# Last stage of a four-layer audio tower: GpSimd without the wait for the mixed heads' norm ahead of its second rest

## The reference, cut to what matters

```python
sx = einsum('bsh,ndh->bnsd', x, hl_w) + hl_b
q = einsum('bnsd,neod->bneso', sx, wq);  k = ...;  v = ...
att = softmax(einsum('bnesd,bntd->bnest', q, k) * d ** 0.5 + causal)
qkv = where(pad, 0.0, einsum('bnest,bntd->bnesd', att, v))
mixed = einsum('bnsed,bnse->bnsd', out, softmax(gates))
hn = layernorm(mixed + resid, ln_g, ln_b)          # the mixed heads' norm
fx = f_n.reshape(b, s, nh, d)
hx = relu(where(fx == 0, 0.0, fx @ fc1_w.T + fc1_b))
hx = where(fx == 0, 0.0, hx @ fc2_w.T + fc2_b)
hx = layernorm(hx + fx, fnorm_g, fnorm_b)          # the second norm
return h + hx * softmax(hx @ fgate_w.T)
```

## Time and profile before

| | |
|---|---|
| median of three runs | 3182.33 us |
| the profiled execution's own time | 3183.66 us |
| its span, first to last instruction | 3181.9 us |
| TensorE busy | 2969.3 us (93%) |
| VectorE busy | 2585.7 us (81%) |
| ScalarE busy | 1806.3 us (57%) |
| GpSimd busy | 1307.3 us (41%) |
| last stage, full rounds | about 2080 to 3040 us, 35 us each |
| draining rounds | about 3040 us to the end |
| TensorE's granted clock, 2080 to 3100 us | 1.00 |

### The profile page before, as it was taken

One profiled execution on the slowest core, in us unless ns is written; L12 is line 12 of the kernel. 1 busy time (PEld: TensorE's weight loads), 2 busy tenths in 40 slices (PEclk: granted clock), 3 DMA queues, 4 the chain that ended last, 5 costly groups with the idle time before them and its releaser, 6 DMA issues.

```text
span 3181.9 us, 72607 instructions
## 1 busy us (share of the span) xinstructions
PE 2969.3 (93%) x24964; PEld 2136.3 (67%) x24964; DVE 2585.7 (81%) x7699; ACT 1806.3 (57%) x4484; POOL 1307.3 (41%) x1368
## 2 busy tenths in 40 slices
PE   0699999999999979999799999999999999999995
PEld 0488888888888844444577777666666666666663
DVE  4788888888888658887778886688888888888873
ACT  0255555555555535555567775466666666666662
POOL 1435353545454324443100001356555555555542
PEclk9999999999999979999778988899999999999996
DMA  4100000000000000000000001432332233233210
GB/s 149 37 22 17 23 16 23 16 23 16 23 16 16 2 1 1 1 1 1 1 1 2 1 1 19 54 42 41 50 50 42 44 50 46 42 50 50 42 23 4
DMA packets 69714, 84.24 MB, mean 26 GB/s; under 512 B 19592, under 2 KB 64968, under 8 KB 68968
## 3 DMA queue, kind: packets, MB, share of 16 engines
q1 hardware_dynamic: 68328, 79.20, 13.8%
q10 hardware_dynamic: 1024, 0.39, 0.1%
HBM read 29.93 MB, written 3.17 MB: 10 GB/s over the span
## 4 chain that ended last, share of the span: by engine, by line
PE 34%; DVE 13%; POOL 2%; issue 2%; ACT 1%; DMA 0%; SPq 0%; POOLq 0%; DVEq 0%; ACTq 0%
PE psum L2310 4%; PE psum L2296 3%; PE psum L2324 3%; PE psum L2283 3%; PE psum L1641 3%; PE psum L2347 3%; DVE qe_top L2763 3%; PE psum L1670 2%; PE psum L1658 2%; POOL qe_root L3013 2%; DVE qe_y L2741 1%; PE psum L1712 1%; PE psum L1703 1%; PE psum L2259 1%; DVE qe_fo L2741 1%
## 5 line engine op out<-in xcount | busy, mean ns | idle before, releaser
L2763 DVE TENSOR_REDUCE qe_top<-psum 125x1 f32<-125x375 f32 (+2 forms) x896 | 499.4, 596 | 102.5 <-PE psum L2283 101.2
L2570 ACT ACTIVATE qe_E<-psum 125x375 f32<-125x375 f32 (+1 forms) x896 | 454.7, 531 | 210.7 <-PE psum L2283 203.7
L2283 PE MATMUL psum<-bconst 125*125 125x125 bf16 (+2 forms) x1792 | 466.5, 260 | 0.0
L606 PE MATMUL psum<-Q,K 96*125 96x125 f32 (+3 forms) x2304 | 404.4, 311 | 0.5 <-ACT E L817 0.4
L606 PEld LDWEIGHTS psum<-Q,K 96*125 96x125 f32 (+1 forms) x2304 | 334.5, 189 | 24.5 <-issue 1.2
L1156 POOL TENSOR_TENSOR Q<-rot 64x375 f32<-64x375 f32 (+1 forms) x256 | 305.7, 1213 | 71.5 <-DVE rot L957 59.4
L2310 PE MATMUL psum<-qe_Q,qe_K 97*125 97x375 bf16 (+2 forms) x1536 | 316.6, 284 | 5.2 <-DMA qe_Q<-qe_maxT 2.4
L817 ACT ACTIVATE E<-psum 125x500 f32<-125x500 f32 x384 | 226.2, 589 | 165.2 <-PE psum L626 163.9
L2296 PE MATMUL psum<-qe_K,qe_Q 96*125 96x375 bf16 (+2 forms) x1536 | 308.6, 282 | 3.3 <-DVE qe_top L2763 3.1
L812 ACT CAST half_scores<-psum 125x250 bf16<-125x250 f32 x384 | 140.6, 366 | 221.9 <-PE psum L611 194.8
L2283 PEld LDWEIGHTS psum<-bconst 125*125 125x125 bf16 x1792 | 248.6, 139 | 11.4 <-issue 7.7
(11 more groups left out here) (341 smaller groups left out, 7255.1 us busy)
## 6 DMA issues: line engine op xcount, KB each, us to landing
qe_Q<-qe_parts SPq DMA_DIRECT2D x192, 187.5 KB, 4.6
s_row<-scores SPq DMA_DIRECT2D x32, 366.2 KB
qe_K<-qe_parts SPq DMA_DIRECT2D x192, 46.9 KB, 4.5
x_tokens<-x SPq DMA_DIRECT2D x32, 187.5 KB
x_chunks<-x SPq DMA_DIRECT2D x4, 750.0 KB
E<-x SPq DMA_DIRECT2D x4, 750.0 KB
out<-qe_hout SPq DMA_DIRECT2D x32, 93.8 KB
weights<-weights_in SPq DMA_DIRECT2D x1, 2363.5 KB, 24.4
```

The costliest lines, as they stand in the source:

```text
L606: nc.tensor.matmul(out[:, first * TP:(first + n) * TP].rearrange("p (o q) -> p o q", o=n), t.K[0:rows(h), par, h, jt * TP:(jt + 1) * TP], ...
L2283: return nc.tensor.matmul(out, B("ident_b")[0:TP, 0:TP], rhs, start=False, stop=True, skip_group_check=True)
L2570: nc.scalar.activation(E[:, e % 2, a:a + width], bank[0:TP, 4 + n % 2, 0:width], ACT.Exp).then_inc(e_done, 1)
L2763: nc.vector.tensor_reduce(dst, src, AX, ALU.max).then_inc(m_read, 1)
```

## The change

GpSimd's step loses the wait for `fx_ready` between the root of the mixed norm and the second rest. No instruction of any engine is added, removed or moved; only the semaphore wait that the second rest (in the draining rounds, mask 1) carried is gone.

```diff
             def step(r, par):
@@
                 if on[5]:
                     take_root(bs[5], s[5], 0)
-                    yield_port(bs[5])
                 if on[1]:
                     leave_rest(bs[1], s[1], 1)
                     other_parts(bs[1], s[1], 0)
@@
-            def yield_port(b):
-                pool.wait_ge(fx_ready, b + 1)
```

## The result

| | before | changed kernel |
|---|---|---|
| median | 3179.6 us (4 runs) | 3211.65 us (4 runs, three of them 3210.41 to 3211.69) |
| the profiled execution's own time | 3183.66 us | 3211.62 us |
| its span | 3181.9 us | 3209.4 us |
| one full round | 34.97 us | 35.89 us |

The ratio is 1.0086, with a 95% interval from 1.006 to 1.0113: slower by 0.9%. (The two medians lie 32 us apart, the two profiled executions 28.0 us; two of the four runs before were short, 3175.29 and 3176.86 us.) A fourth run of the changed kernel took 4208 us at a granted clock of 0.645 instead of 0.953 and is left out of the ratio. The forecast was 3210 us.

What follows compares the result with a forecast made beforehand. TensorE, with 0.33 us of air a round, and VectorE's steps from root to `neg` were taken as the bound. 26.6 us (full rounds) plus 1.5 us (draining) gave 28 us: 3210 us, range 3188 to 3226 us.

Steps and rivals of the forecast that it cites:

- steps 1 and 2: At the mixed norm's root: second rest starts 0.04 us before L3014's end; VectorE's product ends at 2535.31 instead of 2534.62.
- that rival: VectorE's product starts ahead of GpSimd's rest; `neg` 0.23 us late, 6 us in all, 3189 us; chance 0.10.
- steps 3 and 4: L2995 follows the rest, taking 0.95 us; the write of `fx`, issued behind it, lands 1.33 us late.
- steps 5 and 6: L2996, then the third rest to 2538.00; `neg`, issued behind that rest after two maxima, ends 0.95 us late.
- step 5: GpSimd's L2996 starts at 2536.20, delayed by the tail of `fx`, ends near 2537.15; third rest from 2537.10 to 2538.00.
- The rival in which `neg` slips by one operation more: With `fx` over 0.35 us later than worked out, `neg` meets the second L2995, 1.88 us late: 3236 us; chance 0.10.
- The literal rule: Shared VectorE/GpSimd port lock: the loser has its whole duration left; `neg` 1.49 us late, 43 us in all, 3225 us.
- Nothing gives it back: TensorE waits for `fx`, then `neg` at L2335, which starts 0.95 us late; nothing behind that point recovers it.
- The sum: 26.6 us from 28 full rounds at 0.95 us plus 1.5 us from three draining rounds: 28 us.
- TensorE's air of 0.33 us: TensorE is busy for 34.71 us of a 35.04 us round, so its waits cost time almost one for one.

## Why the prediction was right

**Who wins (steps 1 and 2).** As worked out: the rest 0.04 us before L3014's end, the product held until it ended plus 0.2 us, 1.04 us on average where 1.05 was worked out. The run in which the rest comes second shows that the lead of 0.07 us is the cause, and puts the price of the reverse order at 0.32 us a round, where that rival had 0.23.

**`fx` is held as well (steps 3 and 4).** 1.02 us measured, 1.00 worked out. The run with the wait behind the rest separates the two: one collision gives 0.63 us a round, the second brings it to 0.92.

**`neg` is late (steps 5 and 6).** `neg` took 0.40 us, as expected, and behind the product's issue it ended after 3.70 us instead of 2.83, 0.87 us late where 0.95 was worked out. L2996 took 0.85 us in the row, not the 0.95 that step 5 has for it, so the third rest ended 0.08 us sooner than counted. The rival in which `neg` slips by one operation more did not happen. The literal rule, the loser's whole duration after the winner's end, would have given 1.49 us a round; the measured remainders, 0.20 and 0.21 us, decide against it.

**Nothing gives it back.** So it was: all of the 0.92 us is idle or busy time of TensorE. The waits lie where they were forecast, for `fx` 0.65 us a round and for `neg` 0.41. One was missed: `h1T`, of which I said that it is delayed as long as before, takes 1.13 us in the median instead of 1.03, and TensorE waits for it 0.14 us a round. L2335 is 0.86 us late and L2366 0.91 us. The two errors, 0.08 us too much at `neg` and 0.05 us left out at `h1T`, are small and have opposite signs; that 0.95 comes so near to 0.92 is in part luck.

**The sum.** 28 x 0.924 = 25.9 us against 26.6 worked out. The stretch from the 28th to the last `fx` grew from 136.0 to 138.3 us; less one round's 0.92, 1.4 us belong to the draining rounds, where 1.5 were forecast. Together 27.3 us of the span's 27.5.

**What was not right.** TensorE's air of 0.33 us, read from one round, was taken as all that a round has to give; the mean of 27 rounds is 0.46 us. The version in which the parts wait for `neg` is 0.48 us shorter than before, with 0.19 us of idle time left: 0.27 us came out of the idle time and 0.21 us out of the busy time of the rows, which is therefore no floor. And of GpSimd's chain I said that nobody waits for it. That held for a chain that runs earlier; the three kernels in which its end ran 4 us later lost 4% and more, by waits and by the lower clock together.

## What to carry to other kernels

A wait that seems to cost an idle engine something may be what keeps it out of the way of a busy one: before removing it, lay the two timelines side by side and look at what the other engine runs in the gap. Look for small operations with a median far above their minimum (`neg`: 0.189 against 0.872 us); what stands beside them names the cause, and a wait put in front of just the operation that holds them can gain time where a removed wait loses it. Don't take the whole saving of such an operation for a gain: of the 0.65 us saved at `neg`, TensorE's next step got 0.24. Ahead of moving work to a later place, find its last reader, a transfer above all.

## What the runs showed of the hardware

- A held VectorE operation ends a short time after GpSimd's, longer for more elements: 0.05 us for 48 of them, 0.20 to 0.22 us for 192, 0.39 to 0.40 us for 375 (`h1T` in the earlier trace rows: L2995 ends at 2539.76, `h1T` at 2540.15). It is not its whole duration, 0.36 us for 192.
- A one-input operation is held too: `neg` took 0.19 us with GpSimd idle beside it in all full rounds of six kernels, and 0.85 us in the mean with it busy in the kernel before. The reductions from PSUM took the same 0.54 and 0.67 us in either case.
- The order is settled by as little as 0.07 us between the two starts: in the changed kernel the rest led the product by 0.075 to 0.078 us in 27 full rounds of 27, and the product was held each time; in the earlier trace rows VectorE led by 0.07 us and GpSimd was held.
- The granted clock of TensorE, 1.00 through the full rounds before, fell in the kernels with the parts last: 0.94 over 800 us in the first of them, where TensorE waited about 2 us in each round.
